# Attention stage of a graph network: one more step in eight has its value rows weighed by GpSimd instead of VectorE

## The reference, cut to what matters

```python
score = einsum('ehd,ehd->eh', Q[dst], K[src]) / sqrt(32) + relu(efeat @ W1 + b1) @ W2 + b2
ex    = exp(score - segment_max(score, dst)[dst])
alpha = ex / segment_sum(ex, dst)[dst]
out   = segment_sum(alpha[:, :, None] * V[src], dst) @ Wo + bo
```

## Time and profile before

| | us |
|---|---|
| median of three runs | 5541.65 |
| lowest, highest | 5539.95, 5544.51 |
| the profiled execution: span from first to last instruction | 6401.9 |
| time of that execution outside its span | not in its records |
| attention stage in it (about) | 215 to 3255 |
| message sums in it (about) | 4000 to 6400 |

### The profile page before, as it was taken

The page is one execution under the profiler, slowest core; times in us unless marked ns, Lnnn a source line. Parts: engine busy times, 40 slices in busy tenths (PEclk is TensorE's granted clock), DMA queues, the critical chain, the costliest instruction groups (busy, mean ns, idle before and its releaser), DMA issues. The chain is left out here.

```text
span 6401.9 us, 106223 instructions
## 1 busy us (share of the span) xinstructions
PE 4687.5 (73%) x21476; PEld 2770.0 (43%) x21477; DVE 3466.9 (54%) x7990; ACT 3306.9 (52%) x8030; POOL 3423.4 (53%) x3416
## 2 busy tenths in 40 slices
PE   8788888888888888888789999545554445555555
PEld 5345445454444544445444444233333333333333
DVE  6487778888877887878853333222222222222224
ACT  3477777777777777777544444333333333333332
POOL 0366666666666666666610000466666666666665
PEclk9899999999999999999899999766666666666666
DMA  4466666766666666666644444333333333333334
GB/s 138 148 193 192 189 190 193 198 192 193 186 192 186 196 190 193 190 190 197 185 137 140 141 140 140 111 89 89 89 88 89 89 89 87 90 88 87 89 89 116
DMA packets 551965, 929.49 MB, mean 145 GB/s; under 512 B 112845, under 2 KB 361823, under 8 KB 551904
## 3 DMA queue, kind: packets, MB, share of 16 engines
q0 software_dynamic: 208384, 648.75, 36.3%
q1 hardware_dynamic: 343520, 280.03, 13.7%
HBM read 795.60 MB, written 132.88 MB: 145 GB/s over the span
## 5 line engine op out<-in xcount | busy, mean ns | idle before, releaser
L1006 POOL DMA_INDIRECT kv_rows<-kv_d,idx x1664 | 1751.9, 1053 | 1138.4 <-PE sums L1200 593.1
L1786 PE MATMUL m_sums<-m_rows,m_oh 128*128 x3328 | 1176.7, 512 | 1165.0 <-issue 908.6
L1723 POOL DMA_INDIRECT m_rows<-msg_d,m_idx x1568 | 1499.2, 956 | 854.8 <-issue 464.6
L1766 ACT ACTIVATE m_rows<-m_rows,m_norm 128x256 f32<-128x256 f32 x1568 | 710.8, 500 | 1628.9 <-DMA m_rows<-msg_d,m_idx 1528.2
L1786 PEld LDWEIGHTS m_sums<-m_rows,m_oh 128*128 128x128 f32 x3328 | 800.0, 256 | 1542.1 <-issue 1422.7
L1808 DVE TENSOR_TENSOR agg<-agg,m_sums 128x256 f32 x832 | 349.3, 420 | 1673.7 <-DMA kv_rows<-kv_d,idx 1005.8
L1200 PE MATMUL sums<-kv_rows,onehot 128*128 128x264 f32 x3328 | 984.3, 420 | 47.4 <-ACT onehot L1077 18.5
L1040 ACT ACTIVATE hid<-p_hid,b1s 128x512 f32<-128x512 f32 x784 | 495.6, 683 | 648.0 <-remote 226.9
L1200 PEld LDWEIGHTS sums<-kv_rows,onehot 128*128 128x128 f32 x3328 | 590.0, 197 | 461.8 <-issue 346.0
L1157 PE MATMUL p_q<-shelf,pickT 128*128 x4992 | 718.3, 281 | 56.8 <-ACT pickT L1063 28.2
L1656 PE MATMUL p_m<-wr,h1T 128*128 128x512 f32 x1568 | 710.1, 596 | 0.0
(11 more groups left out here) (194 smaller groups left out, 4459.9 us busy)
## 6 DMA issues: line engine op xcount, KB each, us to landing
msg_d<-msg SPq DMA_DIRECT2D x196, 512.0 KB, 2.9
dsts<-dstrow_d SPq DMA_DIRECT2D x208, 256.0 KB
ef_raw<-in_edge_attr_dram SPq DMA_DIRECT2D x195, 256.0 KB
kv_rows<-kv_d,idx POOLq DMA_INDIRECT x1664
m_rows<-msg_d,m_idx POOLq DMA_INDIRECT x1568
kv_d<-kvo SPq DMA_DIRECT2D x49, 260.0 KB, 2.1
pens<-pens_d SPq DMA_DIRECT2D x104, 96.2 KB
emlp<-mlp_d SPq DMA_DIRECT2D x104, 64.0 KB
```

The source lines that it names most:

```text
L1006: pool.indirect_dma_start(rows[:, u, k, :], None, kv_d[:, :], bass.IndirectOffsetOnAxis(idx[:, half, c:c + 1], 0)).then_inc(gathered[u], 16)
L1723: pool.indirect_dma_start(rows[:, u, k, :], None, msg_d[:, :], bass.IndirectOffsetOnAxis(idx[:, u // HALF, c:c + 1], 0)).then_inc(gathered ...
L1766: last = nc.scalar.activation(rows[:, u, k, :], rows[:, u, k, :], ACT.Copy, scale=norm[:, bass.ds(2 * g + k, 1)])
L1786: last = nc.tensor.matmul(sums[u % BANKS][:, 0:D], onehot[:, u % HOTS, k, :], rows[:, bass.ds(slot, 1), k, :].rearrange("p a d -> p (a d)" ...
```

## The change

```diff
-POOLED = (7,)
+POOLED = (3, 7)
 OWN = [r for r in range(8) if r not in POOLED]
```

## The result

The changed kernel takes 5582.9 us (median of 4 runs, 5581.23 to 5585.45), the kernel before in the same comparison 5542.63: 40 us slower, ratio 1.0071 with a 95% interval of 1.0057 to 1.0085. Forecast were 5543 us in 5512 to 5578 and, as the likeliest case, no difference. The sign went to the first rival.

A forecast was written before the change was run, and what follows sets the result against it. TensorE was taken as nearest its limit in the attention stage (85% busy), VectorE mattering where TensorE waits for it. Removal -1, gathers 0, held rescaling +2 gave +1 us: 5543 us, range 5512 to 5578.

The forecast's parts named there:

- the first rival: Position 4: GpSimd's new window stops VectorE's rescaling or weighing, VectorE reaches position 7 late; 5565 to 5588 us, chance 0.23.
- the cover: VectorE's idle time before the adds of positions 4, 5 and 6, said to use up delays before position 7.
- the term of +2 us for the held operations: Position 4: VectorE's two-SBUF-input operations held by GpSimd's weighing, up to 46.7 us of VectorE time, taken as 2 us.
- the price of a stop: Position 4: VectorE held up in 40 of 90 chunks, 32 at the rescaling, by 1.01 us each.
- the removal: Position 6: VectorE's weighing of step 3 goes, 72.3 us of work; gain 0 to 4.9 us, taken as 1.
- the gathers: GpSimd's next gather starts later in 36 of 90 chunks, 0.33 us in the mean over all; cost 0.
- the wait on the weights: GpSimd's new wait before weighing step 3: weights ready 2.8 us before in the chunk shown; costs nothing.
- the present collision: Rival: step 7's weighing on GpSimd no longer meets VectorE's scan; up to 29.0 us off, 5513 us, chance 0.06.

The follow-up runs named there:

- the removal alone: Kernel before, but nobody weighs step 3, so its rows enter the sums unweighed and that part is left out; 5531.2 us, ratio 0.9979 to before.
- the same change with its stop taken away: Changed kernel with one more wait: GpSimd weighs step 3 only after VectorE's rescaling of position 4; 5541.6 us, ratio 0.9997 to before.
- the first trace of before: Unedited kernel before, the profile the prediction rests on; its execution spans 6401.9 us.
- before, again: Unedited kernel before, profiled once more; one execution of 5539.18 us, 24.16 us a chunk.
- the two memsets: VectorE weighs seven steps as before; GpSimd adds a memset of 528 or 1056 columns where the changed kernel weighs step 3; 5539.3 and 5540.4 us.
- the fastest version: GpSimd weighs steps 6 and 7, where the changed kernel gives it 3 and 7; 5513.6 us, ratio 0.9941 to before.
- the kernel with step 6 alone: GpSimd weighs only step 6, where the kernel before gives it step 7; VectorE weighs 0 to 5 and 7; 5550.1 us, ratio 1.0015.

## Why the prediction was wrong

*Step that failed: the cover.* "VectorE has 0.44 us of idle time before that add, 1.23 at the next (0.69 and 1.49 in the mean), and then position 6 with its 1.28 + 0.70." Those rows were true of their execution and of no ordinary one. On this cover rests the term of +2 us for the held operations, and that is the term that failed: the changed kernel takes 52 us more than the removal alone (5582.9 and 5531.2) and 41 more than the same change with its stop taken away. The prediction placed "most of the difference" of 860 us in the message stage; in fact some 475 us of them lie in the attention stage (4.6 us in each of 103 chunks). In an execution of ordinary length the three idle times are 0.71 us in sum, of which the 0.18 at position 4 is no cover: it is still 0.18 in the changed kernel. What slowed the first profiled execution stays open: its granted clock was 0.96 to 0.97 against 1.00, which is too little for a stage that took 19% longer. VectorE's operations take as long in both, and the waits are longer. ScalarE's before the hidden layer (L1040, eight times a chunk) are an example, from 500 to 2500 us, first in the first trace of before, then in before, again:

```profile
L1040 ACT ACTIVATE hid<-p_hid,b1s 128x512 f32<-128x512 f32 x552 | 349.0, 683 | 450.0 <-remote 165.0 <-issue 123.3 <-PE p_hid L1137 119.7
```
```profile
L1040 ACT ACTIVATE hid<-p_hid,b1s 128x512 f32<-128x512 f32 x660 | 417.9, 684 | 245.9 <-PE p_hid L1137 245.9
```

That is 6.5 and 3.0 us a chunk.

*Step mis-sized: the price of a stop.* Expected were stops in 40 of 90 chunks, 32 of them at the rescaling, by 1.01 us: 0.45 us a chunk. Measured are 78 of 90, 71 of them at the weighing in front of the rescaling, by 1.58 us: 1.32 us a chunk. The prediction had let a running VectorE operation finish and GpSimd wait for it; what is seen is the opposite, below. Its own rows held the case. The first of the long scans starts at 299.65 and takes 1.87 us, and GpSimd's weighing starts 0.24 us after it:

```profile
299.89 1.08 POOL L1012 TENSOR_TENSOR kv_rows<-kv_rows,wgt 128x528 f32<-128x528 f32 x1
```

Half of the 30 long scans of that trace began before GpSimd did, by up to 0.50 us.

Of the 1.32 us, 0.52 was taken by the idle time of position 6, lengthened by the removal (0.89 without a stop, 0.37 with), and 0.21 by that of position 5 (0.25 to 0.05). That leaves some 0.6; the chunk is 0.49 longer than with the removal alone (24.62 and 24.13 over the 90 chunks).

*Held: the removal.* Forecast 1 us with 4.9 at most, measured 12 us: more than its bound, but small against 72, and for the reason given (the time turned into idle time at position 6).

*Held: the gathers and the wait on the weights.* The gathers cost nothing; no product waits for a gather in the changed kernel, and the two memsets, which delay the same gathers, cost nothing. The wait on the weights was rightly put at 0 too: GpSimd waits for them before 2 of its 208 weighings. Still, without its stop the change takes 10 us more than the removal alone, and that is not explained.

*Not there: the present collision.* The prediction expected some 30 long scans as before. There are 6 in the trace of ordinary length and 1 in the changed kernel, so that rival had little to give.

*Held: the mechanism, as a rival.* "VectorE is held up and passes it on", 5565 at half and 5588 in full, chance 0.23; measured 5583. Its condition, less than 1.0 us of idle time at positions 4 and 5 in the timed runs, was the right one to ask for (0.43 us), and the trace of 6402 us could not answer it. That 5583 lies so near its full price is luck: the stops take 1.32 us a chunk, three times the 0.45 that the price counted, and over half of that was covered. The range should have taken in the full price; a trace 16% longer than the timed runs is reason to widen, not to scale.

## What to carry to other kernels

Moving a two-operand operation from VectorE to GpSimd can lengthen VectorE's own work: here its operations with two SBUF operands stood still while GpSimd multiplied, 1.58 us at a time. Before choosing which piece to give away, lay GpSimd's window over VectorE's timetable and look for a stretch without such operations. In the fastest version GpSimd's multiplications lie over 195 products, which read PSUM, and over 203 reductions, which read one SBUF operand, and none of these takes longer for it (0.69 us at most). Small operations are no safe place if they read two SBUF operands: `place` (0.27 us alone) takes up to 1.79 us in the kernel with step 6 alone. Here the choice of the step among equals decided between 5514 and 5583 us. And idle time counts as cover only if it stands in a trace as long as the timed runs: compare span and median first.

## What the runs showed of the hardware that I had not expected

A stopped operation ends at a fixed time after GpSimd's ends, 0.57 us for a weighing, 0.55 for the scan, 0.30 for the rescaling and 0.09 for the small `place`, whenever it began. The stopped weighings and scans began between 0.65 us before GpSimd's record starts and 0.8 after; begun 0.68 us or more before, they ran freely (at 0.64 and 0.65 both happened). (This holds for all but a handful of some 390 stopped operations in six traces.) So a weighing that, by the records, was 90% done when GpSimd started still lost 1.58 us, more than the 1.08 of the multiplication. In the records the first to start is thus not the one that keeps the port.

The exception is the weighing of position 0, which directly follows the scan: begun 0.04 to 0.3 us before GpSimd's, it ran its 0.68 us, and it was GpSimd that took longer, 1.33 to 1.60 instead of 1.08 (in 91 of 104 chunks of before, again). The rescaling directly follows a weighing in the same way, and begun 0.08 us before GpSimd's it was stopped all the same (1502.30 and 1502.38 above). What tells the two apart is open.

The Trainium skill, "SBUF — State Buffer", section "SBUF: two separate sides", has the lock, held for the whole instruction and only against a GpSimd operation that reads, and the memsets agree with it (0.43 us beside 1.00 us of writing). It says that whichever starts first gets the port pair; by the start times of these records that does not hold. A port taken some 0.6 us ahead of GpSimd's recorded start would explain the stopped weighings. It was not tested, and it cannot be the whole of it: where GpSimd waits for the rescaling, the rescaling begins 0.6 us before GpSimd's record and keeps its 0.42 us.
